# Exponentials over two PSUM banks at once, and a new order of key pieces and scores, in a one-core attention and butterfly-FFN kernel

## What is computed

```
xn  = layernorm(x)
qkv = xn @ W_qkv + b_qkv                      # 16 heads of 16 dimensions
A   = softmax(q @ k^T, over the 4096 keys) @ v   # for each batch and head, no scaling
F   = butterfly_down(gelu(butterfly_up(xn @ W_exp + b_exp) + up_bias)) @ W_con + b_con + down_bias
out = x + A + F
```

## Time and profile before

| | |
|---|---|
| median of 3 runs | 5672.61 us (5670.88 to 5674.43) |
| the profiled execution | 5674.86 us |
| its span, first to last instruction | 5673.1 us |
| mean granted TensorE clock | 0.992 |
| busy: PE / DVE / ACT / POOL | 5605.1 (99%) / 4884.6 (86%) / 4977.2 (88%) / 524.8 us (9%) |
| instructions | 97332 |

### The profile page before, as it was taken

The page is one execution under the profiler, slowest core; times in us unless marked ns, Lnnn a source line. Parts: engine busy times, 40 slices in busy tenths (PEclk is TensorE's granted clock), DMA queues, the critical chain, the costliest instruction groups (busy, mean ns, idle before and its releaser), DMA issues. The chain is left out here.

```text
span 5673.1 us, 97332 instructions
## 1 busy us (share of the span) xinstructions
PE 5605.1 (99%) x35880; PEld 2613.5 (46%) x35880; DVE 4884.6 (86%) x9104; ACT 4977.2 (88%) x9651; POOL 524.8 (9%) x482
## 2 busy tenths in 40 slices
PE   8799999999999999999999999999999999999999
PEld 5444444444444444444444444444444444444698
DVE  6689999999999999999999999999999999996233
ACT  3489999999999999999999999999999999999544
POOL 2245564000000000000000000000000000000000
PEclk9889999999999999999999999999999999999999
DMA  8611111000000000000000000000000000000111
GB/s 288 200 43 43 50 54 42 21 21 19 14 16 21 21 21 21 15 21 21 21 18 14 16 21 21 21 20 16 21 21 21 17 12 20 21 21 2 34 44 41
DMA packets 232761, 197.02 MB, mean 35 GB/s; under 512 B 171752, under 2 KB 192616, under 8 KB 220520
## 3 DMA queue, kind: packets, MB, share of 16 engines
q1 hardware_dynamic: 228848, 168.00, 10.4%
q0 software_dynamic: 3456, 23.07, 1.4%
HBM read 128.07 MB, written 60.82 MB: 33 GB/s over the span
## 5 line engine op out<-in xcount | busy, mean ns | idle before, releaser
L646 ACT ACTIVATE probs<-psum 128x512 f32<-128x512 f32 x8192 | 4222.6, 608 | 294.8 <-PE psum L843 292.8
L708 DVE TENSOR_REDUCE maxima<-psum 128x1 f32<-128x512 f32 x6036 | 3966.7, 686 | 364.7 <-PE psum L821 255.6
L821 PE MATMUL psum<-k_rows,q_rows 48*128 48x512 f32 x7042 | 2494.3, 455 | 0.6 <-ACT spill L670 0.6
L857 PE MATMUL psum<-probs,v_cols 128*32 128x512 f32 x16384 | 2184.7, 605 | 0.5
L843 PE MATMUL psum<-q_rows,k_rows 50*128 50x512 f32 x8192 | 2061.2, 424 | 0.0
L821 PEld LDWEIGHTS psum<-k_rows,q_rows 48*128 48x128 f32 x7042 | 1176.6, 184 | 1248.8 <-DVE maxima L704 809.6
L843 PEld LDWEIGHTS psum<-q_rows,k_rows 50*128 50x128 f32 x8192 | 1266.5, 186 | 135.0 <-ACT probs L646 44.5
L704 DVE CUSTOM_DVE_ANT_0 merged<-psum,spill 128x512 bf16<-128x512 f32 x1006 | 684.8, 681 | 2.7 <-issue 1.9
L670 ACT ACTIVATE spill<-psum 128x512 f32<-128x512 f32 x1006 | 601.0, 597 | 23.9 <-PE psum L821 23.6
L857 PEld LDWEIGHTS psum<-probs,v_cols 128*32 128x32 f32 x16384 | 323.3, 108 | 622.0 <-issue 325.8
L821 PEld LDWEIGHTS psum<-k_diff,q_rows 48*128 48x128 f32 x1006 | 184.6, 183 | 843.0 <-DVE maxima L708 787.7
(11 more groups left out here) (94 smaller groups left out, 2067.0 us busy)
## 6 DMA issues: line engine op xcount, KB each, us to landing
q_rows<-q_parts SPq DMA_DIRECT2D x128, 256.0 KB
q_parts<-parts SPq DMA_DIRECT2D x32, 512.0 KB, 6.0
k_parts<-parts SPq DMA_DIRECT2D x32, 512.0 KB, 3.7
k_rows<-k_parts SPq DMA_DIRECT2D x64, 256.0 KB
q_rows<-q_parts SPq DMA_DIRECT2D x128, 128.0 KB
planes<-in_up_planes POOLq DMA_DIRECT2D x10, 1024.0 KB, 11.3
planes<-in_down_planes POOLq DMA_DIRECT2D x10, 1024.0 KB, 5.4
y<-in_x SPq DMA_DIRECT2D x16, 512.0 KB, 6.0
```

Source lines behind the costliest of these rows:

```text
L646: nc.scalar.activation(probs[:, 2 * (u % 2) + half, BANK * g:BANK * g + BANK], ps_s[:, r % 4, :], ACT.Exp).then_inc(s_exp, 1)
L708: nc.vector.tensor_reduce(largest, region(use), axis=AX_X, op=ALU.max).then_inc(s_region_free, 1)
L821: nc.tensor.matmul(region(use_of[n, j]), q_rows[m % 4][lower:lower + ROWS, P * t:P * t + P], keys[lower:lower + ROWS, :], start=True, stop ...
L857: last = nc.tensor.matmul(ps_o[VW * g:VW * g + VW, :], v_cols[:, KT * (head % 2) + UNITS * half + at, :], probs[:, 2 * (u % 2) + half, BAN ...
```

## The change

Three things are changed together, all in the attention block.

1. *Exponentials.* ACT takes the two banks of a pair of scores (both key halves of one query group g) in one ACTIVATE of 2 x 512 columns, from two neighbouring banks of ps_s into the two rows of probs. A unit has 4 of them instead of 8. An exp waits until both scores are there, the scores of a pair wait until the exp two pairs earlier is done, and g = 0 waits for both sums of the unit two before. `SCORE` now alternates the halves within each pair.
2. *Order on PE.* The part for a unit becomes

```diff
--- before.py
+++ after.py
@@ -66,7 +66,7 @@
     HALF_N = N // 2
     HALF_P = P // 2
     UNITS = KT // 2
-    EXPS = QG * KT
+    EXPS = QG * KT // 2
     PIECES = N // BANK
     TILES_ALL = SUPER * QT
     UNITS_ALL = SUPER * UNITS
@@ -439,12 +439,11 @@
         ps_o = psum[:, 7, :]
 
 
-        PIECE = [(1, 0), (1, 1), (0, 0), (1, 2), (0, 1), (0, 2), (1, 3), (0, 3)]
-        DIFFERENCE, MERGED = 3, 6
-
-
-        SCORE = [(r // 2 % 2, 2 * (r // 4) + r % 2) for r in range(2 * QG)]
-        LAST_OF_HALF = [max(r for r in range(2 * QG) if SCORE[r][0] == h) for h in range(2)]
+        PIECE = [(1, 2), (0, 0), (1, 0), (1, 1), (0, 1), (0, 2), (1, 3), (0, 3)]
+        DIFFERENCE, MERGED = 0, 6
+
+
+        SCORE = [(1 - r % 2, r // 2) for r in range(2 * QG)]
 
 
         use_of, by_vector, by_scalar, bank_of, use_before, last_in = {}, [], [], [], [], {}
@@ -464,15 +463,11 @@
                 for what in ("apart", "second"):
                     for pair in (i, i + 1):
                         use((n, what, pair), what == "second")
-        use((PAIRED, DIFFERENCE), False)
         for n in range(PAIRED, TILES_ALL + TURN_TILE + 1):
             if n % QT == TURN_TILE:
                 use(("neg", n // QT - 1), True)
             for j in range(PIECES if n < TILES_ALL else 0):
-                if j != DIFFERENCE:
-                    use((n, j), True)
-                elif n + 1 < TILES_ALL:
-                    use((n + 1, j), False)
+                use((n, j), j != DIFFERENCE)
         vector_uses, scalar_uses = list(accumulate(by_vector)), list(accumulate(by_scalar))
 
         def region(n):
@@ -638,13 +633,12 @@
 
             @block.scalar
             def _(act):
-                def exp(u, r):
-                    half, g = SCORE[r]
+                def exp(u, g):
                     if g == 0 and u >= 2:
-                        act.wait_ge(s_pv, 2 * (u - 2) + half + 1)
-                    act.wait_ge(s_score, 2 * QG * u + r + 1)
-                    nc.scalar.activation(probs[:, 2 * (u % 2) + half, BANK * g:BANK * g + BANK],
-                                         ps_s[:, r % 4, :], ACT.Exp).then_inc(s_exp, 1)
+                        act.wait_ge(s_pv, 2 * (u - 1))
+                    act.wait_ge(s_score, 2 * QG * u + 2 * g + 2)
+                    nc.scalar.activation(probs[:, 2 * (u % 2):2 * (u % 2) + 2, BANK * g:BANK * g + BANK],
+                                         ps_s[:, 2 * (g % 2):2 * (g % 2) + 2, :], ACT.Exp).then_inc(s_exp, 1)
 
                 def minus_k():
                     wait_for_stores(act)
@@ -676,20 +670,14 @@
                 for n in range(PAIRED, AHEAD):
                     rectify(n)
                 act.wait_ge(s_ones_in, 16 * 4)
-                for r in range(QG):
-                    exp(0, r)
-                rectify(AHEAD)
-                for r in range(QG, 2 * QG):
-                    exp(0, r)
+                for g in range(QG):
+                    exp(0, g)
                 for u in range(UNITS_ALL):
+                    if u + AHEAD < TILES_ALL:
+                        rectify(u + AHEAD)
                     if u + 1 < UNITS_ALL:
-                        for r in range(QG):
-                            exp(u + 1, r)
-                    if u + AHEAD + 1 < TILES_ALL:
-                        rectify(u + AHEAD + 1)
-                    if u + 1 < UNITS_ALL:
-                        for r in range(QG, 2 * QG):
-                            exp(u + 1, r)
+                        for g in range(QG):
+                            exp(u + 1, g)
 
             @block.vector
             def _(dve):
@@ -806,8 +794,6 @@
 
                 def piece(n, j):
 
-                    if j == DIFFERENCE:
-                        n += 1
                     if n >= TILES_ALL:
                         return
                     m, t = divmod(n, QT)
@@ -833,14 +819,14 @@
 
                     if u >= UNITS_ALL:
                         return
-                    s, e = u // UNITS, 2 * QG * u + r
+                    s, e = u // UNITS, QG * u + r // 2
                     half, g = SCORE[r]
                     if u % UNITS == 0 and r == 0:
                         pe.wait_ge(s_neg_in, 2 * 16 * (s + 1))
-                    if e >= 4:
-                        pe.wait_ge(s_exp, e - 3)
+                    if e >= 2:
+                        pe.wait_ge(s_exp, e - 1)
                     lower, key = HALF_P * half, P * (u % UNITS)
-                    nc.tensor.matmul(ps_s[:, r % 4, :], k_rows[s // 2 % 2][lower:lower + ROWS + MAX_PARTS, key:key + P],
+                    nc.tensor.matmul(ps_s[:, 2 * (g % 2) + half, :], k_rows[s // 2 % 2][lower:lower + ROWS + MAX_PARTS, key:key + P],
                                      q_rows[s % 4][lower:lower + ROWS + MAX_PARTS, BANK * g:BANK * g + BANK],
                                      start=True, stop=True).then_inc(s_score, 1)
 
@@ -848,15 +834,15 @@
 
                     s, at = divmod(u, UNITS)
                     head = s // 2
-                    if at == 0 and half == 0:
+                    if at == 0 and half == 1:
                         if s > 0:
                             pe.wait_ge(s_o_free, s)
                         pe.wait_ge(s_vc[head % 2], 16 * (head // 2 + 1))
-                    pe.wait_ge(s_exp, 2 * QG * u + LAST_OF_HALF[half] + 1)
+                    pe.wait_ge(s_exp, QG * (u + 1))
                     for g in range(QG):
                         last = nc.tensor.matmul(ps_o[VW * g:VW * g + VW, :], v_cols[:, KT * (head % 2) + UNITS * half + at, :],
                                                 probs[:, 2 * (u % 2) + half, BANK * g:BANK * g + BANK],
-                                                start=(at == 0 and half == 0), stop=(at == UNITS - 1 and half == 1))
+                                                start=(at == 0 and half == 1), stop=(at == UNITS - 1 and half == 0))
                     last.then_inc(s_pv, 1)
 
                 pe.wait_ge(s_k[0], 16 * K_LOADS)
@@ -864,7 +850,6 @@
                 for n in range(PAIRED):
                     for i in range(0, PAIRS_OF_TILE, 2):
                         pairs(n, i)
-                piece(PAIRED - 1, DIFFERENCE)
                 for n in range(PAIRED, AHEAD):
                     if n == QT + TURN_TILE:
                         neg_to_rows(0)
@@ -885,24 +870,21 @@
                     n = u + AHEAD
                     if n % QT == TURN_TILE and n // QT <= SUPER:
                         neg_to_rows(n // QT - 1)
-                    piece(n, 0)
-                    score(u + 1, 0)
-                    piece(n, 1)
-                    score(u + 1, 1)
-                    score(u + 1, 2)
-                    piece(n, 2)
-                    score(u + 1, 3)
-                    sums(u, 0)
+                    for j in range(3):
+                        piece(n, j)
+                    for r in range(QG):
+                        score(u + 1, r)
                     piece(n, 3)
                     piece(n, 4)
+                    sums(u, 1)
+                    piece(n, 5)
                     score(u + 1, 4)
                     score(u + 1, 5)
-                    piece(n, 5)
+                    piece(n, 6)
+                    piece(n, 7)
                     score(u + 1, 6)
                     score(u + 1, 7)
-                    piece(n, 6)
-                    piece(n, 7)
-                    sums(u, 1)
+                    sums(u, 0)
```

## The result

The changed kernel takes 5690.63 us (median of 7 runs, 5688.21 to 5692.82) where the kernel before takes 5672.61 (7 runs, 5668.83 to 5674.64). The ratio is 1.0032, 95% interval 1.0022 to 1.0042: slower by about 0.3%, and clear of the 0.2% bound. The forecast was 5690.

A forecast was written before the change was run, and what follows sets the result against it. Bound: a loop of 4.87 us a unit, three quarters PE and one quarter a round trip through a DVE reduction. 5674.9 + 0 + 0 + 19 - 2 = 5692, given as 5690 us against the median; range 5650 to 5750.

The forecast's parts named there:

- The loop: Ordinary unit: PE group A (nine matmuls) 1.74 us, sums 1.00, group B (seven) 1.13, sums 1.00; 4.87, direct saving zero.
- Part 1's inner waits: Inside the nine-matmul group: p2 at about 0.39 us, rectification 0.54, p3 1.20, p4 1.32; these waits cost nothing.
- ACT's schedule: ACT in one unit: rectification at 0.54 us, exps at 1.03, 1.96, 3.51 and 4.44; idle before exp 2 about 0.6.
- Part 2: Wide exps on ACT: repeating every 0.93 us, lasting 1.06, freeing 0.12 a unit, worth nothing where the loop is elsewhere.
- Part 3: Once-per-super events delaying p1 through DVE: together +0.31 us for each of 62 supers, +19 us.
- The transpose of the sums: After the sums' bank transpose, p1's reduction is first behind it: 0.28 us against 0.13 before, +0.15 per super.
- The turning of the maxima: Start of the nine-matmul group, p1 waiting for old p7's reduction: 0.39 us late against 0.23 before, +0.16 per super.
- Part 4: The 20 units without pieces: 4.04 us each in place of 4.12, about 2 us less in all.
- B (ACT takes over): Rival: loop moves to ACT, at exp 3 and the rectification ahead of p3; 5790 us, halfway 5740; chance 0.16.
- 2.85 + 2x: Loop through ACT in us, x being a wide exp's repeat time: 4.71 at x = 0.93; takes over from x = 1.01.
- C: Rival: no measurable change, the once-per-super delays absorbed by slack in the loop; 5671 us; chance 0.23.
- D: Rival: shorter PE steps in the seven-matmul group, at most 0.06 us a unit, -60 us, 5630 us; chance 0.16.

The follow-up runs named there:

- order_alone: The changed kernel with one 512-column exp for each score, as in the kernel before; 5694.5 us.
- negate_late: The changed kernel with only the three small DVE steps moved behind the reductions of pieces 4, 5 and 6 instead of 1, 2 and 4; 5700.6 us.
- the two extra instructions: The changed kernel with a useless ACTIVATE ahead of each rectification, 5765.4 us; with a second one ahead of exp 3, 6018.6 us.
- wide_alone: The kernel before with only the exps widened to two banks of a pair, scores with alternating halves; 5815.3 us.
- wide_adjacent: wide_alone with the first pair's two scores next to each other on PE and the halves of the pairs swapped; 5663.8 us, 0.9990 of the kernel before.

## Why the prediction was right, point by point

- *The loop.* Right, and shown: group A in the new order is the old chain with other names (1.74 and 1.74), B and the sums are unchanged, and a cut in the one reduction moves both kernels by the same 0.12 to 0.13 us in an ordinary unit.
- *Part 1's inner waits.* Piece 2 at 2514.31 is 0.37 in A (0.39 predicted), the rectification at 0.54, piece 3 at 1.19 (1.20), piece 4 at 1.32 (1.32).
- *ACT's schedule* was wrong in one place that costs nothing. Exp 0 was to start at 1.03, right behind the rectification; it starts at 1.24, 0.08 after the update of its second score. So ACT idles before exp 2 for 0.33 and not the "about 0.6" that was named as a sign (the prediction's own schedule, 1.96 + 1.06 to 3.51, gives 0.49). Exp 2 itself starts at 3.50 (3.51), and the loop through ACT runs through exp 2, not through exp 0.
- *Part 2.* Worth nothing, as predicted for this order; order_alone shows it. Sizes: 0.92 and 1.02 where I had 0.93 and 1.06. The Trainium skill's rule ("ScalarE: Activation LUTs", section "What ACT_TABLE_LOAD costs") gives about 1.04 for one wide ACTIVATE, an estimate from its figures; the trace has 1.02, close to it. By either size the loop through ACT is shorter than the one of 4.87.
- *Part 3, the step that decided the sign.* The sum was right by a balance of details: +0.31 us a super predicted, +0.24 measured. The transpose of the sums was +0.28 (0.25 measured). The turning of the maxima was to cost 0.39 at one place; it cost 0.19 there and 0.16 in the group before, 0.35. The statement that failed is "p6 and p7 in B find their banks free": not in the unit in which `negate` and `high_part` delay piece 4's reduction. In negate_late, where B is free of that wait, A takes 0.49 more; but there the small steps stand closer to piece 7's reduction, so the 0.39 by itself was never measured.
- *Part 4.* Units without pieces: 4.04 predicted. The sums stand at 5223.83 and 5227.88 in the changed kernel, 4.05.

```profile
5223.83 1.06 PE L843 MATMUL psum<-probs,v_cols 128*32 128x512 f32 x8
...
5227.88 1.06 PE L843 MATMUL psum<-probs,v_cols 128*32 128x512 f32 x8
```

- *The rivals.* B (ACT takes over) did not happen here, but its formula 2.85 + 2x holds, as the two extra instructions show, and it is what happened in wide_alone, by a wait that I had not seen. C is out: 5690 is beyond 0.2%. D is out: B still takes 1.12 to 1.13, and from sums to sums its median is 2.131 where it was 2.126.
- *What stayed luck.* The forecast hit to 1 us with two terms off by 4 to 6: 0.07 us too much for each of 62 supers, set off by the 0.006 us by which the ordinary units differ. Why they differ is open, and no reading of one unit could have given it. The runs narrow it a little: the median is 4.867 in order_alone, without wide exps, and in wide_adjacent, with the old order of pieces, so neither part is needed for it.

## What to carry to other kernels

When a rotation of few buffers is fed by one engine and emptied by another, the group that asks for the same buffer twice can set the pace, and reordering within it changes nothing as long as a piece and the one that takes its buffer, here three places later, both stay in it; look for the one instruction whose shortening helps (one reduction of seven gave 2% here), not for the busiest engine. Small once-per-block steps belong where their engine's next result is awaited last, and two delays seen in neighbouring groups should be moved together before they are judged. With matmuls in separate halves of the array, put those whose results one consumer needs next to each other in the program.

## What was not expected of the hardware

In these traces matmuls in opposite row halves start ahead of others that stand before them in the program, but are told to waiting engines in the program's order. In wide_alone two scores are over at 2511.56, the update of the second comes at 2511.85, behind piece 1's at 2511.82, and ACT starts at 2511.94; with the same matmuls in another order it starts 0.83 after the group's start instead of 1.10. The Trainium skill says both things ("TensorE: Matmul & The Clock Gate"): that matmuls complete in program order (section "The cost: per-tile semaphore tail"), which agrees with the two runs; and that they stay in program order altogether, with only weight loads pulled ahead (section "Step-by-step: what each phase is for"), with which the rows of wide_alone do not agree: both scores of the pair have started before piece 1 does, though the second stands behind it. I had relied on the early start alone when I expected 5670 us of wide_alone.
